# Third stage of a transformer block: the norm-scale product on VectorE, and GpSimd's scatters issued around the next quad's inverse root

## The reference

```python
y = _layer_norm(x + _mha(x, Wqkv, bqkv, Wo, bo), g1, be1)
idx = jnp.argmax(xf @ Wg.T, axis=-1)                  # one of 8 experts per token
h = jax.nn.relu(xf @ W1[e] + b1[e])
out = out + m * (h @ W2[e] + b2[e])                   # for the token's own expert e
z = _layer_norm(y + _moe(...), g2, be2)
x = x + gb * z                                        # for each token, the result
```

## Time and profile before

| what | us |
|---|---|
| median of 3 runs | 1230.87 |
| lowest and highest of them | 1227.66, 1237.46 |
| the profiled execution, its own time | 1231.36 |
| its span in the profile | 1229.5 |
| VectorE's and GpSimd's part of the third stage | about 1054 to 1221 |

### The profile page before, as it was taken

The page is one execution under the profiler, slowest core; times in us unless marked ns, Lnnn a source line. Parts: engine busy times, 40 slices in busy tenths (PEclk is TensorE's granted clock), DMA queues, the critical chain, the costliest instruction groups (busy, mean ns, idle before and its releaser), DMA issues. The chain is left out here.

```text
span 1229.5 us, 49591 instructions
## 1 busy us (share of the span) xinstructions
PE 1100.4 (90%) x17491; PEld 898.8 (73%) x17491; DVE 955.1 (78%) x4158; ACT 924.4 (75%) x3416; POOL 874.2 (71%) x705
## 2 busy tenths in 40 slices
PE   4699999999999999999999999948998873699991
PEld 2588888888888888888888887626877762688881
DVE  6788898998898898898988987546877754277763
ACT  3689989989989889899899897746866651466660
POOL 3777877877877877778777775554666677178885
PEclk7999999999999999999999999969988975799996
DMA  5776666766766666666767667362242124575100
GB/s 178 207 175 163 177 168 166 183 165 163 182 165 172 174 167 168 176 162 173 177 153 185 162 158 181 79 202 77 78 126 81 67 81 163 155 201 147 57 32 25
DMA packets 110724, 180.50 MB, mean 147 GB/s; under 512 B 19678, under 2 KB 63873, under 8 KB 110352
## 3 DMA queue, kind: packets, MB, share of 16 engines
q1 hardware_dynamic: 102640, 158.14, 49.9%
q0 software_dynamic: 6400, 16.82, 3.8%
q10 hardware_dynamic: 1440, 2.36, 0.8%
HBM read 34.81 MB, written 24.73 MB: 48 GB/s over the span
## 5 line engine op out<-in xcount | busy, mean ns | idle before, releaser
L593 POOL TENSOR_TENSOR qk<-mm,sw 128x1024 f32<-128x1024 f32 x128 | 304.3, 2378 | 102.8 <-DMA sw<-mm 102.5
L673 ACT ACTIVATE pr<-sm,mn 128x96 f32<-128x96 f32 x1024 | 368.6, 371 | 0.3 <-DVE mn L490 0.3
L599 POOL TENSOR_TENSOR pr<-pr,ri 128x768 f32<-128x768 f32 x128 | 189.5, 1480 | 67.9 <-DVE ri L517 67.2
L478 DVE TENSOR_TENSOR mm<-bank,cos 128x512 f32<-128x512 f32 x256 | 175.3, 685 | 72.9 <-PE bank L321 60.2
L673 ACT ACTIVATION_READ_ACCUMULATOR pr<-sm,mn 128x1 f32 x1024 | 202.1, 197 | 0.0
L490 DVE CUSTOM_DVE_ANT_0 sm<-bank,msk 128x96 f32<-128x96 f32 x1024 | 190.9, 251 | 3.7 <-PE bank L347 3.7
L479 DVE TENSOR_TENSOR mm<-bank,sin 128x512 f32<-128x512 f32 x256 | 174.0, 680 | 0.0
L374 PE MATMUL bank<-pT,vw 96*64 96x64 f32 x4096 | 148.3, 226 | 0.0
L374 PEld LDWEIGHTS bank<-pT,vw 96*64 96x64 f32 x4096 | 130.6, 138 | 17.2 <-issue 6.0
L664 ACT ACTIVATE pT<-bank 96x512 f32<-96x512 f32 x256 | 137.3, 588 | 0.0
L389 PE MATMUL bank<-ident,pr 128*96 128x128 f32 x1024 | 132.7, 272 | 0.0
(11 more groups left out here) (201 smaller groups left out, 2489.6 us busy)
## 6 DMA issues: line engine op xcount, KB each, us to landing
sw<-mm SPq DMA_DIRECT2D x512, 128.0 KB, 2.4
vw<-vn SPq DMA_DIRECT2D x128, 192.0 KB, 2.6
vw<-vn SPq DMA_DIRECT2D x128, 128.0 KB, 2.4
rr<-sorted_scratch SPq DMA_DIRECT2D x72, 192.5 KB, 2.7
vw<-vn SPq DMA_DIRECT2D x96, 64.0 KB, 2.3
xt<-in_x SPq DMA_DIRECT2D x16, 256.0 KB, 4.1
x_scratch<-x SPq DMA_DIRECT2D x16, 256.0 KB, 2.6
rr<-x_scratch SPq DMA_DIRECT2D x16, 256.0 KB, 3.2
```

The source lines that it names most:

```text
L478: dve.tensor_tensor(mm[s % 2][:, 0, j, :], PJ[u % 2][:, :], cos[:, :], ALU.mult)
L593: pool.tensor_tensor(qk[i % 2][:, :, 32:], mm[i % 2][:, 0, :, :], sw[i % 2][:, :, :], ALU.add)\
L599: pool.tensor_tensor(t, t, ri[i % 2][:, :].unsqueeze(2).to_broadcast([P, 8, WK]), ALU.mult)\
L673: ins = act.activation(pr[i % 2][:, h, p, :], ms_[i % 2][:, h, p, :], ACT.Exp, scale=-1.0, bias=mn[i % 2][:, h, p:p + 1], accum_out=sums[i ...
```

## The change

The product `yg` of a quad moves from GpSimd to VectorE, behind the bias addition of the quad's tile k = 2. Its waits move with it. GpSimd keeps the roots and the scatters, in a new order: three scatters of quad q - 1, the root of quad q, and the fourth scatter. The wait for `s_zx`, which stood behind the root, now stands ahead of it.

```diff
@@ -972,17 +972,16 @@
                             ap=slot[:, t:t + 1].bitcast(U32), axis=0), in_=quad_rows(u)[:, k, :], in_offset=None,
                             bounds_check=NE * STR - 1, oob_is_err=False).then_inc(s_sca[u % 4], 16)
 
-            def residual(q):
-                pool.wait_ge(s_xs[q % NX], 64 * (q // NX + 1))
-                if q >= 2:
-                    pool.wait_ge(s_ux, q - 1)
-                pool.tensor_tensor(yg[q % 2][:, :, :], xs[q % NX][:, :, 0:C], bc[:, 0:1, :].to_broadcast([P, 4, C]),
-                                   ALU.mult).then_inc(s_yg, 1)
-
-            residual(0)
+            def scatter(w, k):
+                pool.indirect_dma_start(out=out[:, :], out_offset=bass.IndirectOffsetOnAxis(
+                    ap=xs[w % NX][:, k, IX:IX + 1].bitcast(U32), axis=0), in_=ox[w % 3][:, k, :], in_offset=None,
+                    bounds_check=NB * T - 1, oob_is_err=False).then_inc(s_fin[w % NF], 16)
+
             for q in range(NQX + 1):
-                if q + 1 < NQX:
-                    residual(q + 1)
+                if q >= 1:
+                    pool.wait_ge(s_zx, q)
+                    for k in range(3):
+                        scatter(q - 1, k)
                 if q < NQX:
                     pool.wait_ge(s_sx, 4 * q + 4)
                     if q >= 2:
@@ -992,12 +991,7 @@
                     pool.wait_ge(s_rx, 2 * q + 2)
                     pool.tensor_tensor(xrs[q % 2][:, :], xrs[q % 2][:, :], xnh[:, :], ALU.pow).then_inc(s_rx, 1)
                 if q >= 1:
-                    w = q - 1
-                    pool.wait_ge(s_zx, w + 1)
-                    for k in range(4):
-                        pool.indirect_dma_start(out=out[:, :], out_offset=bass.IndirectOffsetOnAxis(
-                            ap=xs[w % NX][:, k, IX:IX + 1].bitcast(U32), axis=0), in_=ox[w % 3][:, k, :], in_offset=None,
-                            bounds_check=NB * T - 1, oob_is_err=False).then_inc(s_fin[w % NF], 16)
+                    scatter(q - 1, 3)
             for h in range(NF):
                 pool.wait_ge(s_fin[h], 64 * len(range(h, NQX, NF)))
 
@@ -1477,6 +1471,12 @@
                     if q >= 4:
                         dve.wait_ge(s_fin[(q - 4) % NF], 64 * ((q - 4) // NF + 1))
                     dve.tensor_tensor(o[:, :, :], z[:, :, :], x[:, :, XC:XC + C], ALU.add).then_inc(s_zx, 1)
+                if k == 2 and 0 <= q < NQX:
+                    dve.wait_ge(s_xs[q % NX], 64 * (q // NX + 1))
+                    if q >= 2:
+                        dve.wait_ge(s_ux, q - 1)
+                    dve.tensor_tensor(yg[q % 2][:, :, :], xs[q % NX][:, :, 0:C], bc[:, 0:1, :].to_broadcast([P, 4, C]),
+                                      ALU.mult).then_inc(s_yg, 1)
                 if k == 3 and 0 <= q < NQX:
                     dve.wait_ge(s_b2b, 4 * q + 4)
                     dve.wait_ge(s_yg, q + 1)
```

## The result

The median of 10 runs is 1243.47 us (1236.72 to 1245.51), against 1231.19 us (10 runs) for the kernel before. The ratio on record is 1.0071, with a 95% interval from 1.0051 to 1.0092; that of the two medians alone would be 1.010. The ten runs lie in two groups, four from 1236.7 to 1239.1 and six from 1243.2 to 1245.5, and the profiled execution, 1243.77, is of the upper one. The forecast was 1238.5 us, 0.6% above the profiled execution of before.

The account below looks back on a forecast made before the run. GpSimd was taken to pace the third stage at 8.21 us a cycle, PE close behind. First root at 1071.03 plus 17 cycles of 8.69, then 9.3, 8.5 and 1.9, gave 1238.5 us; range 1228 to 1249.

Parts of the forecast that it names:

- The ring: Third stage: root, normalization, addition, three scatters and next root wait in a circle; cycle 8.69 us, 0.48 more than before.
- R to Z: From the start of a quad's root (R) to the end of the addition releasing its scatters (Z): unchanged, 4.37 us.
- Z to the next root: From the releasing addition's end to the next root's start: release, three scatters and their issue gaps, 4.32 us.
- The release: On GpSimd, from the addition's end to the first scatter's start: 0.44 us, bounds 0.20 and 0.69.
- The first scatter: First of three scatters ahead of the root, lengthened by the product on VectorE: 1.32 us, bounds 0.97 and 1.47.
- The scatter beside the product: First scatter starts amid VectorE's product and loses the remaining 0.39 us less 0.13: 0.26 us.
- The pace below: PE's own pace in the third stage, read from its early tiles: 7.97 us a quad.
- VectorE's chain: VectorE's work per cycle without idle time: 7.25 us, or 7.96 with the product.
- The end: Last root to the end of the last scatter: 9.3 us against 11.75, only one older scatter being left over.
- rival 2: Relieving GpSimd wins: ring 8.08 us or PE's 7.97, time 1228.1 or 1226.2 us; chance 0.12.
- Rival 3: First two scatters both meet wide VectorE operations: cycle 9.32, time 1249.2 us; chance 0.20, including cases between it and forecast.
- Rival 1: The product does not hold up the first scatter, which lasts 1.08: cycle 8.45, time 1234.4 us; chance 0.18.

Follow-up runs that it names:

- experiment 1: Against the kernel before, only the product moves to VectorE, GpSimd's order stays old: median 1226.84 us against 1232.83, ratio 0.994.
- experiment 4: The changed kernel with 16 of 18 products left out, later additions using old values: one run, 1243.10 us, cycle 8.72 us.
- experiment 5: The changed kernel with four scatters ahead of the root instead of three: one run, 1263.24 us, cycle 10.13 us.
- experiment 6: The changed kernel with two scatters ahead of the root and two behind it: 1226.21 us against 1232.83, ratio 0.9945.
- experiment 3: The changed order, product on GpSimd behind the fourth scatter, held by one more wait until VectorE's normalization is done: one run, 1258.76 us, cycle 9.61 us.
- experiment 2: Against the kernel before, only GpSimd's order changes; the product stays on GpSimd, behind the fourth scatter: 1269.48 us, ratio 1.0296, cycle 10.54 us.
- experiment 7: Two scatters ahead of the root and two behind, with 16 of 18 products left out: one run, 1225.70 us, typical cycle 7.90 us.

## Why the prediction was right

- *The ring.* Root, normalization, addition, three scatters, next root: it is what the timeline shows, and experiments 1, 4, 5 and 6 separate it from VectorE's load. With 0, 2, 3 and 4 scatters ahead the cycles are 7.9, 7.9, 8.71 and 10.13; the ring sets in once it exceeds PE's pace.
- *R to Z.* 4.37 was said; 4.38 is measured.
- *Z to the next root.* 4.32 was said and 4.33 measured, but the terms differ, and that they cancel is in part luck. The release was taken as 0.44 and is 0.80 in every cycle: this is the term that was mis-sized. The first scatter was taken as 1.32 and lasts 0.97. Both were named as signs of being right (a start at 0.3 to 0.5 us, a duration of about 1.3), and both signs failed.

  The cause of the first error can be read: the scatter's own issue work begins with a register move on GpSimd's queue. The first line below, from the changed kernel's rows of L976, dates the first move at 1079.3, when the first L1473 ended (1079.29), and its scatter starts at 1080.1.

```profile
L976 POOLq MOVE  x72: 29/29/29, 1079.3 to 1229.1; - x72
L976 POOL DMA_INDIRECT out<-h,rr x72: 966/969/1152, 1080.1 to 1232.1; - x72
```

  In a row of scatters this work runs under the scatter before, and only 0.30 shows. In the second-stage row that the prediction used, part of it had run ahead of the release: the first move there is at 1026.2, before the `slot` conversion ended at 1026.57, and from that move to the scatter at 1027.01 it is again 0.8 us.

```profile
L971 POOLq MOVE  x4: 29/29/29, 1026.2 to 1027.9; - x4
```

- *The scatter beside the product.* The second error follows for the most part from the first. The meeting priced at 0.26 didn't come about, since with a release of 0.80 the first scatter starts only as the product ends (1115.09); the rest is a scatter of 0.97 where 1.08 was taken ahead of the loss. (1.08 and 0.26 would be 1.34; the sum used 1.32.) The 1.08 was read behind another kind of instruction; experiment 5 shows 1.09 and 0.97 for the two cases. The price itself is right where the two meet, as experiment 1 shows. But it has a limit, which the earlier trace rows don't show and experiment 4 does:

```profile
1113.97 0.75 DVE L1483 TENSOR_TENSOR h<-h,hc 128x512 f32<-128x512 f32 x1
1114.00 0.97 POOL L976 DMA_INDIRECT out<-h,rr  x1 [2.46 <-DVE h L1473]
...
1210.20 0.69 DVE L1483 TENSOR_TENSOR h<-h,hc 128x512 f32<-128x512 f32 x1
...
1210.56 1.18 POOL L976 DMA_INDIRECT out<-h,rr  x1 [2.46 <-DVE h L1473]
```

  A scatter that starts 0.03 us behind the wide addition loses nothing, and one in the same place of the program that starts 0.36 behind it does. So it isn't the wait ahead of the scatter that spares it, but where the scatter starts. In the third stage of all nine traces 114 scatters start 45 ns or more behind the start of such an operation (128x512, two inputs) and at least 0.15 us ahead of its end, and all 114 are lengthened; the 104 that follow a scatter at the usual 0.30 lose what is left of the operation less 0.11 to 0.13 us. Another 44 start at most 34 ns behind it, or up to 12 ns ahead, and last 0.97 to 1.02. Why the limit lies there the traces don't show.

  The Trainium skill, "SBUF — State Buffer", section "Who interferes with whom", infers that `tensor_tensor` leaves the generation of descriptors alone. The 114 lengthened scatters speak against that inference. Its rule that GpSimd and VectorE block each other by whole instructions, by the order in which they issue, fits those scatters, if the order of issue turns between 34 and 45 ns of the recorded starts, and experiment 3 (1.54 us). Experiment 2 (2.88 us) it doesn't explain as recorded, since there the operation that was held up had started first.
- *The pace below.* PE's 7.97 a quad, read from its early tiles, is a typical 7.90 in experiments 6 and 7, or 7.94 as the mean without the two short last cycles. VectorE's chain was put at 7.96 as well; experiment 6 has three cycles of 7.83 or 7.84 with it, so that sum was about 0.1 too long.
- *The end.* Last root to last scatter: 9.3 said, 9.57 measured; the difference is again the longer release (0.79 for 0.44) less the shorter first scatter (0.97 for 1.08).
- *The sum.* The profiled execution is 1243.77, 5.3 us above the forecast: 3.9 are the later first root, 0.8 the cycles, 0.3 the end, 0.3 the time outside the span. The later first root also takes the last one to 1223.5, just outside the 1214 to 1223 that were named. Of the 0.8, 0.6 are in one cycle of 9.32, where GpSimd stood 0.89 us between two scatters with nothing to wait for. It is the 13th of the 17, and the same cycle is 0.5 to 0.6 us longer than its neighbours in experiments 2 to 5 too, so it is no stray; its cause stays open.
- *The rivals.* The relief (rival 2) needed Z to root under 3.9. With two scatters ahead GpSimd could start the root 3.06 us behind Z, and there the gain comes at once. Rival 3 didn't happen. Rival 1's condition, no loss to the product, did hold, but with the longer release its cycle is that of the forecast. The measurement so supports the ring and doesn't tell the forecast's first scatter from rival 1's; the timeline does, and it is nearer to rival 1.

## What to carry to other kernels

Taking work off the engine that paces helps only if the new order doesn't close a ring: before a wait is moved ahead of something, write down who waits for what is queued behind it, and add up the ring in the timeline's durations, with the release of each wait in it. The two halves of this change had opposite signs (0.994 and, by the cycles, 8.71 against 8.21), so they are worth timing apart; one scatter fewer ahead of the root made the whole a gain of 0.55%.

## What the runs showed of the hardware

- In the third stage, an indirect DMA of GpSimd that stands behind a wait starts 0.79 to 0.82 us behind the release, in every cycle of the seven kernels in which that wait holds it up, while a VectorE result reaches a waiting GpSimd root in 0.1 us (experiment 6). On the ring such a DMA costs 0.5 us more than one that follows another at 0.30.
- Such a DMA that starts 45 ns or more behind the start of a 128x512 VectorE operation with two inputs is lengthened by about what is left of it less 0.12 us (114 of 114); one that starts at most 34 ns behind isn't (44 of 44).
- GpSimd's 1.20 us product stretched VectorE's four normalizing operations from 1.12 to 2.88 us when it was queued directly behind a scatter (experiment 2), and a single two-input multiplication from 0.68 to 1.54 us (experiment 3). Idle time on GpSimd was no free place for it: 2.46 us were idle, and the product there cost 1.83 us a cycle.
